# Attention output: where the third column block of the output bank is added

## The reference

```python
qkv = jnp.einsum('bse,ef->bsf', x, W_qkv)
q, k, v = ...
q = rotary_embedding(q, seq_len, HEAD_DIM)
k = rotary_embedding(k, seq_len, HEAD_DIM)
scores = jnp.einsum('bqhd,bkhd->bhqk', q, k) * scale
scores = jnp.where(mask, scores, NEG_INF)
weights = jax.nn.softmax(scores, axis=-1)
out = jnp.einsum('bhqk,bkhd->bqhd', weights, v)
```

## Time and profile before

| | |
|---|---|
| median of 3 runs | 2729.64 us (2729.27 to 2730.74) |
| profiled execution | 2724.24 us, its span 2722.5 us |
| mean granted TensorE clock | 0.987 |
| TensorE busy | 2588.0 us, 95% |
| VectorE busy | 2075.0 us, 76% |
| ScalarE busy | 1617.1 us, 59% |
| GpSimd busy | 1500.1 us, 55% |

### The profile page before, as it was taken

How to read it: one execution, slowest core, us unless ns; L and a number is a source line. 1 busy time by engine, 2 the same in 40 slices (tenths; PEclk the granted TensorE clock), 3 DMA queues, 4 the chain that set the end, 5 groups by cost and what they waited for, 6 DMA issues and landing times. The chain is left out here.

```text
span 2722.5 us, 50823 instructions
## 1 busy us (share of the span) xinstructions
PE 2588.0 (95%) x16671; PEld 2292.4 (84%) x16671; DVE 2075.0 (76%) x4468; ACT 1617.1 (59%) x3152; POOL 1500.1 (55%) x1673
## 2 busy tenths in 40 slices
PE   7999999999999999999998799999969999999998
PEld 5888888888888888888887688888869999999997
DVE  6878888888887888887878688988856666666664
ACT  3666666666666666767666433333336666666664
POOL 3676756776656666577653444444434444444443
PEclk9999999999999999999999899999979999999999
DMA  6644454444543545453435665555344443444433
GB/s 176 121 123 117 102 136 109 117 111 118 132 103 100 134 103 125 104 123 90 106 81 124 177 180 144 159 149 142 104 136 108 105 104 56 107 108 102 106 54 47
DMA packets 192048, 316.16 MB, mean 116 GB/s; under 512 B 60048, under 2 KB 105776, under 8 KB 188784
## 3 DMA queue, kind: packets, MB, share of 16 engines
q1 hardware_dynamic: 149200, 217.90, 32.4%
q0 software_dynamic: 42656, 95.88, 14.4%
HBM read 237.41 MB, written 75.17 MB: 115 GB/s over the span
## 5 line engine op out<-in xcount | busy, mean ns | idle before, releaser
L1212 ACT ACTIVATE a_pt<-a_PT 128x512 fp32r<-128x512 f32 (+3 forms) x768 | 350.0, 490 | 390.3 <-PE a_PT L1067 384.3
L1359 DVE TENSOR_TENSOR a_pt<-a_PT,a_pt 128x512 fp32r<-128x512 f32 (+3 forms) x768 | 400.4, 548 | 117.3 <-ACT a_pt L1212 112.8
L1349 DVE CUSTOM_DVE_ANT_0 a_S<-a_S,a_mask 128x1024 f32<-128x1024 f32 (+7 forms) x512 | 386.4, 755 | 31.4 <-PE a_S L1056 30.4
L1201 ACT ACTIVATE a_pb<-a_S,a_nmax 128x1024 f32<-128x1024 f32 (+7 forms) x512 | 380.5, 743 | 40.6 <-DVE a_nmax L1349 39.3
L1067 PE MATMUL a_PT<-early_ident,a_pb 128*128 128x128 f32 x2304 | 339.6, 274 | 47.3 <-DVE a_pt L1359 43.7
L1067 PEld LDWEIGHTS a_PT<-early_ident,a_pb 128*128 128x128 f32 x2304 | 271.7, 141 | 103.6 <-issue 62.8
L1088 PE MATMUL a_O<-a_pt,a_v 128*128 128x256 f32 x2048 | 331.0, 289 | 13.9 <-DVE a_ot L1379 6.6
L1088 PEld LDWEIGHTS a_O<-a_pt,a_v 128*128 128x128 f32 x2048 | 282.0, 192 | 28.0 <-DVE a_xt L1334 11.0
L2343 POOL DMA_INDIRECT early_stage<-in_we,e_ix x116 | 130.8, 1127 | 260.0 <-issue 140.2
L1055 PE MATMUL a_S<-a_kh,a_qs 128*128 128x512 f32 (+3 forms) x768 | 270.7, 352 | 0.9 <-ACT a_pb L1201 0.9
L1056 PE MATMUL a_S<-a_kl,a_qs 128*128 128x512 f32 (+3 forms) x768 | 256.6, 346 | 0.0
(11 more groups left out here) (334 smaller groups left out, 7714.2 us busy)
## 6 DMA issues: line engine op xcount, KB each, us to landing
a_qs<-early_rot SPq DMA_DIRECT2D x256, 128.0 KB, 2.4
a_kh<-early_rot SPq DMA_DIRECT2D x256, 128.0 KB, 2.6
a_kl<-early_rot SPq DMA_DIRECT2D x256, 128.0 KB, 2.3
m_hn<-scr_hs SPq DMA_DIRECT2D x39, 516.0 KB, 3.7
scr_attT<-a_ot SPq DMA_DIRECT2D x256, 64.0 KB, 2.1
early_stage<-in_wqk POOLq DMA_DIRECT2D x31, 512.0 KB, 4.0
m_att<-scr_attT SPq DMA_DIRECT2D x30, 512.0 KB, 4.5
m_rb<-scr_rinv SPq DMA_DIRECT2D x60, 256.0 KB, 5.5
```

The source lines that it names most:

```text
L1201: act.activation(pb[u % 2][:, 0:cols], S[u % 2][:, 0:cols], ACT.Exp, bias=nmax[:, u % GU:u % GU + 1], scale=-1.0, accum_out=rsum[:, b % 2, ...
L1212: act.activation(pt[u % 2][:, 0, 4 * s:4 * s + m, (qt % 2) * P:(qt % 2 + 1) * P], PT[(k + s) % 2][:, 0:m * P].rearrange("p (k q) -> p k q" ...
L1349: dve.tensor_tensor_reduce(out=sc, in0=sc, in1=mask[:, T - cols:T], scale=-1.0, scalar=-MASKED, op0=ALU.add, op1=ALU.min, accum_out=nmax[: ...
L1359: dve.tensor_tensor(pt[u % 2][:, 1, 4 * s:4 * s + m, q], PT[(k + s) % 2][:, 0:m * P].rearrange("p (k q) -> p k q", k=m), pt[u % 2][:, 0, 4 ...
```

## The change

`out_low` gets a second copy ahead of its own: block 2 of the upper partitions goes to SBUF, to the right half of the pair's `ot` buffer, which serves as scratch. It waits for the store that last read this buffer, as `out_add` did. `out_add` loses the reduce. It waits for both copies, adds the scratch to the right half of `otmp` in SBUF, and then adds blocks 0 and 1, now side by side, to `otmp` as before. `s_otmp` counts two for each pair.

```diff
             def out_low(k):
                 act.wait_ge(s_pv, k + 1)
+                if k >= 4:
+                    act.wait_ge(s_ost[k % 4], 16 * (k // 4))
+                act.activation(ot[:, k % 4, P:2 * P], O[0:HD, 2 * P:3 * P], ACT.Copy).then_inc(s_otmp, 1)
                 act.activation(otmp[:, :], O[HD:P, 0:2 * P], ACT.Copy).then_inc(s_otmp, 1)
...
             def out_add(k):
-                dve.wait_ge(s_pv, k + 1)
-                dve.tensor_reduce(O[0:HD, 3 * P:4 * P], O[0:HD, P:3 * P].rearrange("d (a t) -> d t a", a=2), AXX,
-                                  ALU.add).then_inc(s_olo, 1)
-                dve.wait_ge(s_otmp, k + 1)
+                dve.wait_ge(s_otmp, 2 * k + 2)
+                dve.tensor_tensor(otmp[:, P:2 * P], otmp[:, P:2 * P], ot[:, k % 4, P:2 * P], ALU.add).then_inc(s_olo, 1)
                 dve.wait_ge(s_olo, k + 1)
-                if k >= 4:
-                    dve.wait_ge(s_ost[k % 4], 16 * (k // 4))
-                dve.tensor_tensor(ot[:, k % 4, :].rearrange("d (a t) -> d a t", a=2),
-                                  O[0:HD, :].rearrange("d (a t) -> d a t", a=4)[:, 0:4:3, :],
-                                  otmp[:, :].rearrange("d (a t) -> d a t", a=2), ALU.add).then_inc(s_ofree, 1)
+                dve.tensor_tensor(ot[:, k % 4, :], O[0:HD, 0:2 * P], otmp[:, :], ALU.add).then_inc(s_ofree, 1)
```

## The result

| four runs each | before | after |
|---|---|---|
| median | 2730.16 us (2729.27 to 2730.74) | 2866.91 us (2863.75 to 2875.15) |
| ratio | | 1.0509, 95% interval 1.0490 to 1.0528 |
| span of the profiled execution | 2722.5 us | 2867.2 us |
| mean granted TensorE clock | 0.987 | 0.971 |

The account below looks back on a forecast made before the run. TensorE was taken to bound the attention stretch, idle mostly when VectorE is late. Slips of 29 + 3 + 20 + 5 = 57 us, less 10, gave +47: 2771 profiled, 2777 as median; range 2736 to 2825.

Parts of the forecast that it names:

- given back: TensorE's slips let VectorE catch up and take up part of its 74 us idle time: 10 us off.
- What bounds, and where it reaches TensorE: TensorE sets the pace in the attention stretch; only third and fourth pairs without slack count: 57 us before the deduction.
- The cost of each instruction: Per pair: new VectorE add 0.28 us, new ScalarE copy 0.28, removed reduce 0.42, last add unchanged at 0.42.
- The chain: From products to free bank, 0.94 us becomes 1.5; +0.65 where ScalarE's copy was last, as at 31 third pairs.
- The lock at fourth pairs: At 14 value-weight fourth pairs the add waits for GpSimd's 2.40 us subtraction; TensorE slips 1.4 us each, 20 us.
- The lock at third pairs: At 31 third pairs without slack, the new add waits 0.27 us on average for the running GpSimd instruction.
- The lock elsewhere: Some 0.1 us at 33 other third pairs, 3 us; 0.13 at some 35 late fourth pairs, 5 us.
- Rival 1: The lock does not bite the 64-partition or short add; only third pairs slip: +10 us, 2740; chance 0.15.
- Rival 2: VectorE's 0.14 us relief per pair shortens TensorE's wait for the low parts: faster, 2712 to 2722; chance 0.05.
- Rival 3: VectorE becomes the bound: 187 us extra occupancy, half reaching TensorE, +93 us, 2823; chance 0.17.
- Rival 4: Nothing to measure: third-pair slips of 9 us less the 10 that come back, 2729; chance 0.08.
- What would show it: Adds spread up to 2 us, ending with GpSimd's; output-product idle up some 30 us; ScalarE's waits and later work unchanged.

Follow-up runs that it names:

- the kernel with the scratch in the bank: Changed kernel, but block 2 is copied to block 3 of the output bank, so the short add has one PSUM input: 2744.3 us, ratio 1.0073.
- the lock at k modulo 16 = 10: Changed kernel with block 2 copied within the output bank, except at k modulo 16 = 10, where the copy goes to SBUF: 2805.7 us, ratio 1.0282.
- the kernel with three reduces: Kernel before, with three extra 1024-column VectorE reduces ahead of the last add at k modulo 16 = 10: 2801.5 us, ratio 1.0266.
- the kernel with gaps: Changed kernel, but GpSimd waits for its own result behind each rotary low part (L881): 2805.9 us, ratio 1.0291.

## Why the prediction was right in direction and wrong in size

From the ratios, against the kernel with the scratch in the bank, the parts are:

| part | forecast | measured |
|---|---|---|
| longer chain and second copy | 20 of the third pairs' 29 | 20 |
| lock at third pairs, k modulo 16 = 10 | with the next | 57 |
| lock at the other third pairs (what is left) | 31 x 0.27 = 8.4 | 22 |
| lock at fourth pairs with a value weight | 20 | 23 |
| lock at all other pairs | 3 + 5 = 8 | 16 |
| given back | -10 | nothing to be seen |
| sum | 47 (46.4 with these rounded terms) | 138 (medians: 137) |

The row of 22 us is a remainder, 0.0509 less 0.0073, 0.0209, 0.0086 and 0.0059; no kernel had these pairs alone, and by the intervals it can be off by 16 us. In the traces it lies at five third pairs at k modulo 16 = 2, held for 3.3 to 4.1 us in the changed kernel: TensorE's idle time before their output products is 15.5 us longer in sum than with the scratch in the bank, and slower work comes on top. At the remaining third pairs the difference is under 0.3 us in sum.

- **What bounds, and where it reaches TensorE.** Right. The wait for the bank at third and fourth pairs took nearly all the idle time, as the prediction placed it, and the work behind the attention phase changed by under 4 us of 1200.
- **The cost of each instruction.** Right: 0.28 us for the add without a wait, 0.26 for the copy.
- **The chain.** Right in kind; that 31 x 0.65 = 20 us equals the 20 measured with the scratch in the bank is in part luck. The 31 products slipped by 0.47 us each, 15 us; the other 5 us came elsewhere. The 10 us taken off for idle time that would be taken up came back in no kernel: L1067's idle time of 47.3 us is 46.2 with the scratch in the bank, 44.9 with the lock at k modulo 16 = 10, and 52.2 in the changed kernel.
- **The lock at fourth pairs.** Right, in mechanism and size. There the wait was read from one row, with the instruction's own start and end.
- **The lock at third pairs: the step that failed.** The prediction took "a random arrival waits 0.66 x 0.4 = 0.27 us" for the 31 third pairs without slack, 8 us in sum. In the changed kernel the new adds at these 31 are held for 57 us in sum, 1.85 us each. The mean over all 256 was not the trouble: it is 0.45, near the 0.43 that the prediction kept for the range. Two things are wrong in the step. The arrival isn't random. The order of work repeats every 16 pairs, and each engine comes to this point from its own full queue, so they meet at the same point again and again: 11 of the 16 adds at k modulo 16 = 10 are held for over 3 us. At 13 of the 16 long holds GpSimd had last waited for another engine some 5.8 us before, for VectorE's rotary product (L1325), and had then run L874, L875, L859, a DMA issue (L853) and L881 one after the other. The trace of the kernel before has the meeting already: at exactly these 16 third pairs the first of the two L881 begins between 0.11 us ahead of VectorE's last add and 0.35 us behind it. And the wait doesn't end with one instruction if others follow without a gap. Signs of both stood in the earlier trace rows: L881 from 418.24, "just as the new add would", is there as x2 with 2.56 us. The text read from it "1.3 more", one instruction, and then put the mean in the sum all the same. The row's own value for 16 places, 2.5 us or more, would have made 40 us of idle time from the 8.
- **The clock: a term that was missing.** The 43 us more of busy time are what half speed behind the long idle times costs. It isn't proportional: 16 idle times of 1.1 us cost 2 us of it, 16 of 3.3 us cost 26. Between these it went either way: the clock fell behind all three idle times of 1.9 us in the kernel before, and behind none of three of 1.8 us in the kernel with three reduces. A forecast that has single delays of several us on TensorE's path needs this term. It could be read before: in the earlier trace rows the five products behind 1.88 us of idle time take 1.28 us, in the earlier trace rows 0.86, and the kernel before has there (TensorE busy throughout, clock 0.51)

```profile
373.10:376.50 3.40, 3.40 (x18) 3.40 (x18) 3.40 (x6) 1.92 (x4) 3.32 (x4) 0.51 0.85 265
```

- **The lock elsewhere.** 8 forecast, 16 measured. The difference is mostly runs of two instructions again, at three first pairs.
- **The rivals.** Rival 1, no lock, falls. Rival 2, a gain, falls: VectorE lost 0.14 us per pair and nothing came of it. Rival 3 named a size nearer to the truth, but its mechanism, VectorE as the bound, isn't what happened: VectorE is busy 1257.3 of 1582 us, 79%, against 82% before, its busy time grew by 83 us where the rival had 187, and few places carry the cost. Rival 4, nothing to measure, falls too.
- **What would show it.** The adds ending with GpSimd instructions, the 14 of 2 us and the unchanged rest came as named. "Up to 2 us" was exceeded twofold, and TensorE's idle time before the output products grew by 81 us, not by "some 30". "ScalarE's own waits should not grow" failed: the exponentials' wait for the row maximum went from 39.3 to 118.3 us, and only to 52.4 with the scratch in the bank. The row maximum of first and third pairs stands behind the held add in VectorE's queue.

The Trainium skill (SBUF — State Buffer, section "Who interferes with whom") says of the lock that whoever issues first gets the shared pair of ports for the whole instruction. The held adds bear out the second half, with 64 partitions too. The first half doesn't fit the recorded starts: the add at 445.91 began ahead of L881 at 446.02 and took 3.97 us, not 0.28, and in the last section an instruction of VectorE that began second went first. The recorded start may not be the moment at which an engine asks for the ports; no run shows that moment. So the measurement decides, and the page says nothing of a run of instructions.

## What to carry to other kernels

Before an elementwise instruction on VectorE gets a second SBUF input, look up what GpSimd does at the very places where somebody waits for it. Take the recorded starts of both engines there, not a mean, and price the worst case as the whole run of GpSimd instructions up to the next gap; one input left in PSUM made the same add free of it (1.0073 against 1.0509). Engines that go through the same schedule over and over don't meet at random: what meets at one repetition meets at most of them. And price a delay on TensorE's path by its size at each place: here delays of about 1 us cost what they last, and delays of 3 to 4 us cost half as much again, because the clock falls behind them.

## What the runs showed of the hardware

**Runs of GpSimd instructions keep VectorE out, but not always.** Nineteen adds waited through two or three instructions that follow each other at once. Eleven of them began 0.06 to 0.2 us before the first of these, all while GpSimd was issuing a DMA (L853); whether that plays a part wasn't tried. Others got in between two such instructions. This add at k = 42, VectorE and GpSimd, is one:

```profile
342.30 0.34 DVE L1376 TENSOR_TENSOR a_otmp<-a_otmp,a_ot 64x128 f32<-64x128 f32 x1 [1.73 <-ACT a_otmp L1221]
...
341.22 2.56 POOL L881 TENSOR_TENSOR early_rot<-early_stage,early_rot 128x512 fp32r<-128x512 f32 x2
```

It began 0.2 us before the first L881 ended and was done 0.15 us behind that end. In the changed kernel all adds that began within the last 0.44 us of such an instruction got in. The nineteen began earlier than that, or before the run. But one add that began 1.86 us before the end of an L951, with another L951 directly behind, got in at that end too (k = 252):

```profile
1647.86 2.00 DVE L1376 TENSOR_TENSOR a_otmp<-a_otmp,a_ot 64x128 f32<-64x128 f32 x1 [1.75 <-ACT a_otmp L1221]
...
1645.00 7.09 POOL L951 TENSOR_TENSOR early_xT<-early_stage,early_xT 128x1024 fp32r<-128x1024 f32 x3
```

So how long before the end it begins isn't the rule, and what decides was not settled. That a small gap lets VectorE in is shown by the kernel with gaps.

**GpSimd can lose as well.** One add (k = 6) that began together with L874 ran ahead of it in 0.28 us, and L874 took 1.43 us instead of 1.29. And here an instruction of VectorE with two SBUF inputs and 128 partitions began 0.3 us behind GpSimd's:

```profile
402.50 1.21 DVE L1311 TENSOR_TENSOR early_xT<-early_stage,early_xT 128x1024 fp32r<-128x1024 f32 x1
...
402.19 2.43 POOL L939 TENSOR_TENSOR scan_keys<-scan_k,a_coef 128x512 f32<-128x512 f32 x1
```

VectorE's took its own 1.2 us, and L939 took 2.43 us where its median is 1.05. The same happened at the two other places where these two meet.

**A GpSimd instruction that didn't hold the add.** L896, a tensor_scalar over 128x512 in SBUF, did not in its last 0.6 us. VectorE and GpSimd:

```profile
200.21 0.28 DVE L1376 TENSOR_TENSOR a_otmp<-a_otmp,a_ot 64x128 f32<-64x128 f32 x1
...
198.74 2.09 POOL L896 TENSOR_SCALAR a_xt<-a_xt,a_mv,a_nw 128x512 f32<-128x512 f32 x1
```

The add ran wholly inside the last 0.6 us of L896, and took 0.28 us. It was so for all nine adds that ran wholly inside L896. All nine began about 0.6 us before its recorded end, so what its earlier part does isn't shown. All 120 adds that were held stood beside GpSimd's tensor_tensor instructions, of one elementwise operation on two tensors. Whether the number of inputs is what matters wasn't tried.
